# Post-norm decoder layer with a mixture of experts: expert outputs added by the scatter into the residual rows

## What is computed

```python
for e in range(E):
    match = topk_experts == e
    elig = match.any(-1) & ~fallback
    pos = jnp.cumsum(elig) - 1
    kept, overflow = elig & (pos < cap), elig & (pos >= cap)
    ...
    y_e = _ffn(x_flat[idx], W1[e], b1[e], W2[e], b2[e])
    w = jnp.where(valid, w_tok[idx], 0.0)
    y_flat = y_flat.at[idx].add(y_e * w[:, None])
    y_flat = jnp.where(overflow[:, None], y_fb, y_flat)
    fallback = fallback | overflow
x = _layernorm(x + y_flat)
```

## Time and profile before

| | us |
|---|---|
| median of 3 runs | 1519.68 (1519.27 to 1520.58) |
| time of the profiled execution | 1522.42 |
| its span, first to last instruction | 1520.6 |
| TensorE busy | 1343.9 (88%) |
| VectorE busy | 1113.7 (73%) |
| ScalarE busy | 925.7 (61%) |
| GpSimd busy | 730.0 (48%) |

### The profile page before, as it was taken

How to read it: one execution, slowest core, us unless ns; L and a number is a source line. 1 busy time by engine, 2 the same in 40 slices (tenths; PEclk the granted TensorE clock), 3 DMA queues, 4 the chain that set the end, 5 groups by cost and what they waited for, 6 DMA issues and landing times. The chain is left out here.

```text
span 1520.6 us, 48478 instructions
## 1 busy us (share of the span) xinstructions
PE 1343.9 (88%) x17429; PEld 1126.0 (74%) x17429; DVE 1113.7 (73%) x3110; ACT 925.7 (61%) x2255; POOL 730.0 (48%) x923
## 2 busy tenths in 40 slices
PE   3599989999999999999999999873899999999940
PEld 2478878888888888888888888641588888888820
DVE  4588878888888888888888889748455555555537
ACT  3566768777777777877777766623344444444426
POOL 3144564575575566566656644520244334444336
PEclk9799999999999999999999999995899999999975
DMA  9667666766757666666676664109532263323235
GB/s 219 127 155 162 164 149 164 143 137 179 143 132 186 138 143 162 155 145 143 167 146 135 156 112 88 26 15 411 165 79 74 77 157 98 76 77 76 74 134 208
DMA packets 293219, 209.01 MB, mean 137 GB/s; under 512 B 218782, under 2 KB 250654, under 8 KB 290560
## 3 DMA queue, kind: packets, MB, share of 16 engines
q1 hardware_dynamic: 281952, 184.01, 51.3%
q0 software_dynamic: 6816, 17.71, 3.9%
q10 hardware_dynamic: 4224, 4.19, 0.8%
HBM read 93.79 MB, written 65.93 MB: 105 GB/s over the span
## 5 line engine op out<-in xcount | busy, mean ns | idle before, releaser
L1635 PE MATMUL ps_e<-xt,wres 128*128 128x128 f16 x3408 | 343.4, 220 | 5.6 <-DMA xt<-xg 4.8
L1635 PEld LDWEIGHTS ps_e<-xt,wres 128*128 x3408 | 285.5, 98 | 77.6 <-issue 6.2
L1699 ACT ACTIVATE act_g<-ps_e,b 128x128 f32<-128x128 f32 x568 | 162.7, 369 | 207.8 <-PE ps_e L1635 207.6
L1642 PE MATMUL ps_e<-wres,g_hi 128*128 x568 | 214.5, 379 | 0.8 <-DVE g_lo L1722 0.8
L707 ACT ACTIVATE probs<-st_k,nmax 128x128 f32<-128x128 f32 (+1 forms) x512 | 199.6, 447 | 2.0 <-DVE nmax L914 1.9
L914 DVE CUSTOM_DVE_ANT_0 st_k<-ps,causal 128x128 f32<-128x128 f32 (+1 forms) x512 | 160.5, 351 | 35.6 <-PE ps L432 35.6
L1602 POOL DMA_INDIRECT z_scr<-e_y,dst_i x71 | 85.9, 1209 | 209.4 <-DVE e_y L1713 207.6
L714 ACT ACTIVATE pt_hi<-ps 128x384 f16<-128x384 f32 x256 | 125.0, 488 | 54.1 <-PE ps L440 31.8
L1644 PE MATMUL ps_e<-wres,g_lo 128*128 x568 | 154.8, 273 | 0.0
L1180 POOL TENSOR_TENSOR o_st<-o_norm,o_st 128x256 f16<-128x256 f32 x128 | 86.2, 673 | 133.6 <-ACT o_st L722 130.8
L1710 DVE SCALAR_TENSOR_TENSOR e_y<-ps_e,b 128x256 f32<-128x256 f32 x71 | 30.1, 424 | 158.9 <-PE ps_e L1644 158.9
(11 more groups left out here) (270 smaller groups left out, 4240.7 us busy)
## 6 DMA issues: line engine op xcount, KB each, us to landing
k_pair<-k_pair SPq DMA_DIRECT2D x96, 256.0 KB, 6.4
st_p<-in_moe_w SPq DMA_DIRECT2D x24, 768.0 KB, 6.2
w_scr<-st_p SPq DMA_DIRECT2D x24, 768.0 KB, 4.4
wres<-w_scr SPq DMA_DIRECT2D x18, 1024.0 KB, 21.6
v_scr<-v_tok SPq DMA_DIRECT2D x32, 512.0 KB, 3.8
v_pos<-v_scr SPq DMA_DIRECT2D x64, 256.0 KB, 6.2
q_st<-st_q SPq DMA_DIRECT2D x64, 128.0 KB, 3.4
z_scr<-zero SPq DMA_DIRECT2D x32, 256.0 KB, 3.6
```

The source lines that it names most:

```text
L1635: last = mm(out, w(c * FF + f * P, b, P), xt[:, t % X_BUFS, a, c], start=(m == 0), stop=(m == 5))
L1642: mm(out[:, 0:2 * D], g_hi[:, t % G_BUFS, f], w(KC * FF + f * D, 0, 2 * D), start=(f == 0), stop=False, skip_group_check=True)
L1699: nc.scalar.activation(act_g[:, k % 2, f], ps[:, 3 + 2 * (k % 2) + f // 4, (f % 4) * P:(f % 4 + 1) * P], ACT.Gelu, bias=bias[:, f:f + 1], ...
```

## The change

The result rows no longer go to a place for each choice. z_scr is now the residual: attention stores x2 there (rows 0 to 4095), and 128 spare rows behind them are set to zero by one store in step 4, instead of all 8192 rows in steps 0 to 3. dst_i is the token itself, or the spare row 4096 + partition for an empty slot; a new table, second, holds which choice a slot is.

In the experts block, once the shares are final, SP stores them as a table of 8192 numbers in x2_scr (share_table), between its transposes 0 and 1; VectorE computes for each slot its place in the table (share_rows, four instructions). For each tile GpSimd gathers 128 numbers from it (share_in). The eviction of a tile has three instructions: the two of before write to y_part, the third multiplies by the slot's share and writes y. TensorE waits for y_part. The scatter has compute_op=add, has no bounds check, and waits until the scatter before it has landed. SP's residual loads are gone.

The final block loads 8 groups of 512 KB from z_scr, 4 KB in one piece for each partition, which now holds tokens 32p to 32p+31. VectorE takes statistics from the loaded rows, GpSimd does only the power, ScalarE normalises in place, SP issues the stores.

```diff
-        def zeros(n):
-            if n == 0:
-                sp.wait_ge(s_const, N_FILLED)
-            z = io["z_scr"].rearrange("(p n) d -> p (n d)", p=P)
-            part = z.shape[1] // ZERO_STEPS
-            for at in range(n * part, (n + 1) * part, 2 * D):
-                sp.dma_start(z[:, at:at + 2 * D], zero[:]).then_inc(s_z_out, 16)
+        def spare_rows():
+            sp.wait_ge(s_const, N_FILLED)
+            sp.dma_start(io["z_scr"][TOKENS:TOKENS + P, :], zero[:]).then_inc(s_z_out, 16)
...
-            sp.dma_start(io["x2_scr"][bass.ds(t * P, P), :], x2[:, p]).then_inc(s_out_x2[p], 16)
+            sp.dma_start(io["z_scr"][bass.ds(t * P, P), :], x2[:, p]).then_inc(s_out_x2[p], 16)
...
+def share_table(io):
+
+    return io["x2_scr"][0:CODES // D, :].rearrange("n d -> (n d)").rearrange("(n a) -> n a", a=1)
...
+        def share_in(t):
+            if t == 0:
+                pool.wait_ge(s_table, 16)
+                pool.wait_ge(s_row, 4)
+            if t >= 2:
+                pool.wait_ge(s_in[t % 2], 16 * (t // 2))
+            nc.gpsimd.indirect_dma_start(share_of[:, t:t + 1], None, share_table(io),
+                                         bass.IndirectOffsetOnAxis(ap=share_at[:, t:t + 1].bitcast(U32), axis=0)).then_inc(s_in[t % 2], 16)
+
+        def add_rows(t):
             pool.wait_ge(s_ye, t + 1)
+            if t >= 1:
+                pool.wait_ge(s_sc, 16 * t)
             nc.gpsimd.indirect_dma_start(io["z_scr"], bass.IndirectOffsetOnAxis(ap=dst_i[:, t:t + 1].bitcast(U32), axis=0), y[:, t % 2], None,
-                                         bounds_check=CODES - 1, oob_is_err=False).then_inc(s_sc[t % 2], 16)
+                                         compute_op=ALU.add).then_inc(s_sc, 16)
 
         for k in range(-3, N + LAG):
             if k + 3 < N:
                 gather(k + 3)
+            if 0 <= k < N:
+                share_in(k)
             if k >= LAG:
-                scatter(k - LAG)
-        for q in range(2):
-            pool.wait_ge(s_sc[q], 16 * ((N + 1 - q) // 2))
+                add_rows(k - LAG)
+        pool.wait_ge(s_sc, 16 * N)
...
-                    pe.wait_ge(s_ye, k - LAG - 1)
+                    pe.wait_ge(s_y_part, 2 * (k - LAG - 1))
...
+        turn(0)
+        table_out()
+        for t in range(1, N):
             turn(t)
-            if 0 <= t - 28 < TILES // FINAL_Q:
-                residual(t - 28)
...
+            dve.wait_ge(s_y_part, 2 * t + 2)
+            dve.wait_ge(s_in[t % 2], 16 * (t // 2 + 1))
             if t >= 2:
...
+                dve.wait_ge(s_sc, 16 * (t - 1))
+            nc.vector.tensor_scalar(y[:, t % 2], y_part[:, 1], share_of[:, t:t + 1], None, ALU.mult).then_inc(s_ye, 1)
...
         for n in range(N):
-            sp.dma_start(z[:, n], io["z_scr"].rearrange("(t p k) d -> p t k d", p=P, k=2)[:, n * Q:(n + 1) * Q]).then_inc(s_z[n], 16)
+            sp.dma_start(x2[:, n], io["z_scr"][0:TOKENS].rearrange("(p t) d -> p t d", p=P)[:, n * Q:(n + 1) * Q]).then_inc(s_z[n], 16)
+        for n in range(N):
+            sp.wait_ge(s_n, (n + 1) * Q)
+            sp.dma_start(io["out"].rearrange("(p t) d -> p t d", p=P)[:, n * Q:(n + 1) * Q], x2[:, n]).then_inc(s_out, 16)
+        sp.wait_ge(s_out, 16 * N)
...
-            dve.wait_ge(s_b, n + 1)
+            dve.wait_ge(s_z[n], 16)
             for j in range(Q):
-                nc.vector.scalar_tensor_tensor(out=z[:, n, j, 1], in0=z[:, n, j, 1], scalar=w[:, 1, n * Q + j:n * Q + j + 1],
-                                               in1=x2[:, n, j], op0=ALU.mult, op1=ALU.add).then_inc(s_s, 1)
-            for j in range(Q):
-                dve.wait_ge(s_s, n * Q + j + 1)
-                nc.vector.bn_stats(stats[:, p, j], z[:, n, j, 1]).then_inc(s_st, 1)
+                nc.vector.bn_stats(stats[:, p, j], x2[:, n, j]).then_inc(s_st, 1)
```

More of the change, by code:

```diff
@@ L50 @@
 PAIRS = H // 2
-ZERO_STEPS = 4
+ZERO_STEP = 4
 V_LOADS = 2
@@ L1360, in routing_block @@
     te_pack = sb("te_pack", [P, SLOT_TILES // PACK], F32)
+    spare = sb("r_spare", [P, 1], F32)
+    second = keep["second"]
     s_const = sem("r_const")
@@ L1535, in _ @@
         link(v.tensor_tensor(tokf[:], pad[:], code[:], ALU.add))
[L1536 to L1541, removed]
+        link(v.tensor_scalar(spare[:], tokens[:, T // 2:T // 2 + 1], float(TOKENS - MIDDLE - 1), None, ALU.add))
+        link(v.tensor_scalar(pad[:], code[:], 0.0, None, ALU.is_equal))
+        link(v.scalar_tensor_tensor(out=dst_i[:], in0=pad[:], scalar=spare[:, 0:1], in1=tokf[:], op0=ALU.mult, op1=ALU.add))
+        link(v.tensor_scalar(second[:], ps[:, 1, SLOT_TILES:2 * SLOT_TILES], 0.0, None, ALU.not_equal))
 FINAL_Q = 4
-FREED = TILES * D * 4 // (2 * WSIZE * 2)
 def experts_block(nc, ctx, io, keep):
@@ L1568, in experts_block @@
     y = sb("e_y", [P, 2, D], F32)
+    y_part = sb("e_part", [P, 2, D], F32)
+    row_i = sb("e_row", [P, 2, SLOT_TILES], I32)
+    row_f = sb("e_rowf", [P, SLOT_TILES], F32)
+    share_at = sb("e_share_at", [P, SLOT_TILES], I32)
+    share_of = sb("e_share_of", [P, SLOT_TILES], F32)
     ps = ctx.enter_context(nc.psum_tensor("ps_e", [P, 8, 512], F32))
     ps_y = [ps[:, 1, :], ps[:, 2, :]]
-    (s_h, s_g, s_g_hi, s_g_lo, s_y, s_yb, s_ye, s_sc0, s_sc1) = [
-        sem("e_" + n) for n in "h g g_hi g_lo y yb ye sc0 sc1".split()]
+    (s_h, s_g, s_g_hi, s_g_lo, s_y, s_yb, s_ye, s_sc) = [
+        sem("e_" + n) for n in "h g g_hi g_lo y yb ye sc".split()]
     s_xt = [sem("e_xt%d" % n) for n in range(X_BUFS)]
-    s_sc, s_ga = [s_sc0, s_sc1], keep["s_ga"]
-    s_share = sem("e_share")
+    s_ga = keep["s_ga"]
+    s_share, s_table, s_row, s_y_part = (sem("e_" + n) for n in ("share", "table", "row", "y_part"))
+    s_in = [sem("e_in%d" % n) for n in range(2)]
     chosen = sb("e_chosen", [P, TILES, E], F32)
@@ L1675, in turn, with table_out @@
             sp.dma_start_transpose(xt[:, t % X_BUFS].rearrange("p k c n -> p (k c) n"), xg[:, t % X_BUFS]).then_inc(s_xt[t % X_BUFS], 16)
[L1677 to L1683, removed]
+        def table_out():
+            sp.wait_ge(s_share, 8)
+            sp.dma_start(share_table(io).rearrange("(p k) a -> p (k a)", p=P), keep["weights"][:].rearrange("p k t -> p (k t)")).then_inc(s_table, 16)
+        turn(0)
+        table_out()
+        for t in range(1, N):
             turn(t)
-            if 0 <= t - 28 < TILES // FINAL_Q:
-                residual(t - 28)
     @block.scalar
@@ L1736, in shares, with share_rows @@
                 dve.wait_ge(s_share, done)
+        def share_rows():
+            nc.vector.tensor_single_scalar(row_i[:, 0], tok_i[:], P - 1, ALU.bitwise_and).then_inc(s_row, 1)
+            nc.vector.tensor_single_scalar(row_i[:, 1], tok_i[:], 7, ALU.arith_shift_right).then_inc(s_row, 1)
+            dve.wait_ge(s_row, 2)
+            nc.vector.scalar_tensor_tensor(out=row_f[:], in0=row_i[:, 0], scalar=float(2 * TILES), in1=row_i[:, 1], op0=ALU.mult,
+                                           op1=ALU.add).then_inc(s_row, 1)
+            dve.wait_ge(s_row, 3)
+            nc.vector.scalar_tensor_tensor(out=share_at[:], in0=keep["second"][:], scalar=float(TILES), in1=row_f[:], op0=ALU.mult,
+                                           op1=ALU.add).then_inc(s_row, 1)
         dve.wait_ge(keep["s_b"], 32)
```

68 lines of the change are left out of this document (20 added, 48 removed).

## The result

The changed kernel takes 1533.83 us, the kernel before 1519.68 on the same chip; the ratio is 1.008, with a 95% interval of 1.006 to 1.010. It is 0.8% slower, clear of the noise, where 1494.2, 1.7% faster, was forecast. The profiled execution of the changed kernel has a span of 1529.2 us, 8.6 more than that of before.

The account below looks back on a forecast made before the run. TensorE was taken to bound the experts and attention (one 4.09 us hole there), the last stage counting by itself. -24.3 - 4.4 + 3.2 = -25.5 off the median 1519.68 gave 1494.2 us, range 1487 to 1515.

Parts of the forecast that it names:

- Last stage: Final block: fewer operations and half the bytes read, bound passing from VectorE to ScalarE's normalisation; 24.3 us gained (22 to 26).
- t0: Start of the last stage's first DMA, 1468.38 us in the profile before; the stage was forecast to end at t0 + 27.9.
- Zero stores: Attention: removing 32 zero stores from SP's queue ends TensorE's 4.09 us wait; 4.4 us gained (0 to 5.5).
- The second rival: Attention: the hole stays, since key moves and weight pieces share the engines; 1498.6 us, chance 0.13.
- the third, transfers that hold the last stage: Final block: loads and stores share bandwidth, 30.5 us instead of 27.9; 1496.8 us, chance 0.1.
- Tail: End of experts: the last adding scatters wait for one another, each landing in 3.8 us; 3.2 us lost (0.5 to 8.6).
- Steady state: Experts: share gather, adding scatter, its wait and VectorE's extra instruction fit under the 5.28 us step; nothing lost.
- First rival, the scatter loop binds: Experts: GpSimd's wait for the preceding scatter exceeds 5.28 us a tile; about 1540 us, chance 0.22, of which 0.18 ends slower.
- The port lock: Experts: VectorE's lock holds up GpSimd's descriptor writing, so most scatters may take about 2 us; sum about 1 us higher.
- The add costs only a second read: Adding scatter: the DMA's add costs no time beyond a second source read; sum some 2 us lower.

Follow-up runs that it names:

- e4: The kernel before with only the first of its 32 stores of zeros to the result rows: 1516.90 us.
- e1: The changed kernel with a plain scatter in place of the adding one, sums over a token's experts lost: 1493.85 us.
- e3: The changed kernel with a plain scatter and without share gathers, outputs neither weighted nor summed: 1487.89 us.
- e2: The changed kernel without its 71 share gathers (shares all 1), adding scatter and its wait kept: 1493.65 us.
- e10: e1 plus a computation of 1.0 us a tile on GpSimd: 1494.36 us.
- e11: The changed kernel without share gathers, plus a computation of 1.0 us a tile on GpSimd in their place: 1493.50 us.
- e20: The whole changed kernel with each share 16 times in the table, so a share gather fetches 64 bytes a partition instead of 4: 1499.47 us.
- e7: The kernel before with an adding scatter and one more unused 4-byte gather a tile, no wait between scatters: 1566.64 us.
- e17: e9 with its second share gather fetching 512 bytes a partition in place of 4: 1495.69 us.
- e5: The kernel before with an adding scatter onto zero rows, no scatter waiting for another: 1520.63 us.
- e13: e1 plus a load of 128 x 4 bytes a tile on SyncE's queue, behind the tile's transpose: 1547.40 us.
- e9: The changed kernel with a plain scatter and a second, unused share gather a tile: 1668.17 us.
- e18: e2 plus an unused gather a tile of 4 bytes a partition, at 64-byte spacing in a 256 KB table in another buffer: 1497.84 us.
- e16: e13 with 512 bytes a partition in place of 4 in the added load: 1495.87 us.
- e8: The changed kernel with share gathers for even tiles only, odd tiles using the shares of the tile before: 1506.03 us.

## Why the prediction was wrong

- *Last stage, -24.3*: right in mechanism and nearly in size, 25.8 measured. The first load took 3.69 (4.2 forecast), ScalarE 16.3 for eight groups (17.0), from t0 to the end 26.4 (27.9). The bound passed to ScalarE as said; the shift took 0.15 as said.
- *Zero stores, -4.4*: right in the place and nearly in size; 3.6 alone (e4), and the wait of 4.09 in front of TensorE's matmul is gone. The second rival, that the hole stays, is out. So is the third, transfers that hold the last stage: ScalarE ran through.
- *Tail, +3.2*: the part that the sum described was nearly right, a landing of 3.65 against 3.8. A wake-up and the issue cost more than the 0.3 (the last scatters start 4.9 and 4.4 us apart, not 4.1). From the 67th scatter (1473.42, before 1446.65) to the drain's start it takes 3.8 us more than before: 2.3 between the scatters, 1.5 from the last one's start to the drain. The term missed GpSimd's drain at the block's end, which had no place in the sum: 6.50 instead of 2.67, another 3.8. (By its own working the lower bound of 0.5 is 1457.2 + 3 x 2.8 + 0.6 - 1466.0 = 0.2.) The drain is longer with either part (4.05 with the adding scatter alone, 8.71 with the plain scatter and the share gathers), but the parts don't add up, and no run shows what sets it. In e1 it is the whole cost: 8.71 - 2.67 = 6.0, and e1 is 6.0 slower than e3.
- *Steady state, "nothing"*: this is the step that failed, by 32 us. GpSimd's queue has three pauses of 0.30 a tile, so its sum was 3.9 to 4.9 and not 3.6 to 4.6, still under 5.28. Otherwise its arithmetic held: the loop of landing and wake-up (4.4 to 5.0 from start to start) stayed under 5.28, and with the adding scatter, VectorE's new instruction and TensorE's wait for y_part all in place e2 has a distance of 5.28: they cost nothing there. The failure is in "share gather the same by analogy (as many descriptors)". I priced the new gather as time in GpSimd's queue, which is right (0.95 us) and harmless (e10, e11). I gave no price to where it reads. The table is 32 KB, all tiles hit it, and with an adding scatter beside it TensorE pauses for 0.4 to 1.2 us at a time; with the same gather from a table 16 times as large (e20) the loss is gone. No row of the kernel before shows a transfer of this kind, so its cost should have been bounded and a rival made of it.
- *First rival, the scatter loop binds*: its sign came true (scatters 5.77 us apart), its mechanism did not: the longest idle times of TensorE end by "issue", not by g_lo or y_part, and e7, without the wait, loses more.
- *The port lock*: the forecast that most scatters would fall on g_lo and take 2 us didn't come true. In the kernel before 14 of 71 scatters take about 2.0 us, the others 1.02. In the changed kernel's order of VectorE's instructions a plain scatter (e1) takes 1182 ns by the median and at most 1253, so the mean is no longer than before, 1.17 against 1.21 us, and with other neighbours in GpSimd's queue it takes 989 (e17). What the 166 ns by the median come from isn't shown. Most of the longer generation is the addition's own: in the old order it goes from 1016 to 1592 ns (e5). The exclusive lock that the Trainium skill, SBUF — State Buffer, section "SBUF: two separate sides", describes for the port pair of VectorE and GpSimd may be behind the 14 scatters of 2 us, but no run isolates it.
- *The add costs only a second read*: in e5 the kernel's time is level with the kernel before (1.000 to 1.002), but the landing is hidden there. The adding scatters land 4.2 us after issue by the median where plain ones take 2.8; 0.6 of the 1.4 more is descriptor generation, the other 0.8 is not taken apart by any run. The Trainium skill, Collectives: The Full Stack, section "The bandwidth ceiling: the fold count and why AG ≠ RS ≠ AR", says that the add itself costs nothing beyond a second source read; these figures fit that and don't show it.

**What stays open.** The runs show that small reads from the small table are necessary for the loss, and that 128 of them a tile are harmless beside plain scatters (e1) and cost 32 us in the steady state beside adding ones. Without any addition, 128 more cost 53 us from 512 bytes on SP's queue (e13) and 174 from the table on GpSimd's (e9). They don't separate the table's size, several entries within 64 bytes, and the pair of 4 bytes and this buffer. Nor do they show how the reads stop TensorE. The records of its instruction transfers, 16 KB each, take no longer in the kernel after than before (median 1.01 and 1.09 us), and the pauses are not tied to them. That instructions and table lie in a part of DRAM where one holds up the other is a guess that these records don't support, and no run moved the instructions. The Trainium skill, DMA: Bandwidth & Descriptors, section "Latency and other measured facts", infers for large power-of-two row pitches that streams pile up on one channel of DRAM; no run here shows it.

## What to carry to other kernels

A small table that every tile looks up need not be a small cost: measure it, and if it costs, spread it (here each entry 16 times, so that entries are 64 bytes apart) or let the value travel in a row that is fetched anyway. When TensorE's idle time is put down to "issue" in the middle of a run of matmuls, look at what else reads DRAM at that time, too, and not only for a semaphore. And price a block's end: GpSimd's drain took 2.67 to 8.71 us in these runs, and no sum had it.

## What the hardware showed beyond what was expected

- 256 reads of 4 bytes a tile from a table of 32 KB cost TensorE 130 us of pauses in e9, while the DMA engines were busy for only 21% of the time. Beside adding scatters one such gather of 128 reads cost 32 us between scatters 1 and 66, and one of as many reads of 4 bytes from a table of 256 KB no pauses (e18, 4.2 us slower than e2, of which 2.5 are the drain).
- A load of 512 contiguous bytes a tile, cut into 128 pieces of 4, cost 1547.4 - 1493.9 = 53.5 us on SyncE's queue; 64 KB in its place cost 2 (e16).
- Two changes that cost 6 us each cost 46 together: taking parts out one at a time would have blamed each for 40.
- GpSimd's drain at the end of a block took 2.67 us after 142 plain gathers and scatters, 4.05 where the scatters add, 8.71 after 213 plain ones and 6.50 after 213 with adding scatters. It doesn't grow with their number alone: after 284 plain ones it took 6.75 (e9, e17), after 178 with adding scatters 3.85 (e8).
